# Value product in halves, causal mask of the probabilities on GpSimd, row maxima over two PSUM banks at once, exponentials from single banks

## The reference

```python
x = L0(x, c)   # quantised products and a gated scan, then an MLP
x = L1(x, c)   # attention, all keys;    then an MLP of width 512
x = L2(x, t)   # two small MLPs
x = L3(x, c)   # attention, causal mask; then an MLP of width 512

# attention in L1 and L3: 16 heads of 8 features
h = layernorm(x) * (1 + scale) + shift
q, k, v = split(h @ Wqkv)
s = q @ k.T / sqrt(8)
s = where(causal, s, -inf)          # L3 only
x = x + gate * (softmax(s) @ v) @ Wproj
```

## Time and profile before

| | us |
|---|---|
| median of 3 runs (495.15 to 497.51) | 497.06 |
| the profiled execution | 498.7 |
| its span | 496.6 |
| mean granted TensorE clock, share of full | 0.931 |
| loop of L1, first E to last copy of bank 6 | 198.1 to 301.5 |
| loop of L3, the same | 378.1 to 473.1 |

### The profile page before, as it was taken

How to read it: one execution, slowest core, us unless ns; L and a number is a source line. 1 busy time by engine, 2 the same in 40 slices (tenths; PEclk the granted TensorE clock), 3 DMA queues, 4 the chain that set the end, 5 groups by cost and what they waited for, 6 DMA issues and landing times.

```text
span 496.6 us, 6007 instructions
## 1 busy us (share of the span) xinstructions
PE 321.8 (65%) x2017; PEld 151.0 (30%) x2018; DVE 311.0 (63%) x787; ACT 242.7 (49%) x422; POOL 108.4 (22%) x160
## 2 busy tenths in 40 slices
PE   0025845621346463877777888867758999999886
PEld 0014523410115320121111224543412333334454
DVE  0778787859688568778888723335666555565230
ACT  3267556552564221466666685342422445555542
POOL 0112149632262510000000040173300000000410
PEclk9999999999999966599999999997965999999899
DMA  7940440000000332000000000000360000000001
GB/s 251 416 165 0 170 176 0 1 0 0 1 0 1 97 94 64 2 0 2 1 3 1 3 2 0 1 0 0 86 170 1 3 2 2 2 2 3 2 1 42
DMA packets 11650, 21.90 MB, mean 44 GB/s; under 512 B 2010, under 2 KB 10462, under 8 KB 10846
## 3 DMA queue, kind: packets, MB, share of 16 engines
q1 hardware_dynamic: 11620, 21.52, 12.6%
HBM read 14.57 MB, written 0.52 MB: 30 GB/s over the span
## 4 chain that ended last, share of the span: by engine, by line
PE 46%; DVE 26%; ACT 11%; issue 8%; POOL 6%; DMA 2%; SPq 0%; DVEq 0%; ACTq 0%; POOLq 0%
PE ps L1455 11%; PE ps L1437 7%; DVE nm L918 7%; PE pe L1477 4%; PE pe L1358 4%; PE ps L1510 4%; PE ps L1442 3%; POOL rstd L341 2%; PE pe L1480 2%; ACT scr L1130 2%; PE ps L1412 2%; DVE st L500 2%; ACT scr L1042 2%; PE ps L1229 1%; DMA big<-in_wa 1%
## 5 line engine op out<-in xcount | busy, mean ns | idle before, releaser
L918 DVE TENSOR_REDUCE nm<-ps 128x1 f32<-128x512 f32 (+2 forms) x224 | 135.0, 648 | 55.8 <-PE ps L1442 34.7
L1155 ACT ACTIVATE scr<-pe 128x1024 f32<-128x1024 f32 (+3 forms) x128 | 108.9, 866 | 102.5 <-PE pe L1480 59.2
L1437 PE MATMUL ps<-big 62*128 62x512 bf16 (+3 forms) x256 | 50.5, 386 | 36.3 <-DVE nm L918 32.6
L1455 PE MATMUL ps<-scr 128*32 128x512 f32 (+3 forms) x512 | 61.3, 552 | 6.2 <-ACT scr L1130 5.4
L341 POOL TENSOR_TENSOR rstd<-var,half 128x4 f32<-128x4 f32 x26 | 28.5, 1098 | 114.2 <-DVE var L505 88.2
L1477 PE MATMUL pe<-big 64*128 64x512 bf16 (+3 forms) x256 | 47.2, 367 | 1.1 <-ACT scr L1155 1.1
L425 POOL CAST nm<-nm 128x16 bf16<-128x16 f32 x16 | 3.2, 198 | 196.7 <-DVE nm L918 196.7
L1437 PEld LDWEIGHTS ps<-big 62*128 62x128 bf16 x256 | 14.5, 96 | 65.9 <-DVE nm L918 49.3
L1477 PEld LDWEIGHTS pe<-big 64*128 64x128 bf16 x256 | 12.5, 95 | 53.3 <-issue 24.9
L1358 PE MATMUL pe<-hT,w 128*128 128x512 f32 x48 | 24.6, 638 | 3.5 <-ACT hT L1109 3.5
L510 DVE TENSOR_SCALAR xn<-x_tok,mv,rstd 128x128 f32<-128x128 f32 x56 | 15.8, 344 | 13.6 <-POOL rstd L341 13.5
(11 more groups left out here) (221 smaller groups left out, 592.9 us busy)
## 6 DMA issues: line engine op xcount, KB each, us to landing
big<-tern SPq DMA_DIRECT2D x48, 128.0 KB, 2.4
big<-in_fill SPq DMA_DIRECT2D x1, 4096.0 KB, 13.6
big<-in_wa SPq DMA_DIRECT2D x1, 2304.0 KB, 12.5
w<-in_w SPq DMA_DIRECT2D x2, 1152.0 KB, 19.3
big<-in_wa SPq DMA_DIRECT2D x1, 1344.0 KB, 6.2
big<-in_w SPq DMA_DIRECT2D x1, 1024.0 KB, 14.3
w<-in_w SPq DMA_DIRECT2D x1, 896.0 KB, 20.0
rowg<-in_rowg SPq DMA_DIRECT2D x1, 832.0 KB, 18.3
```

What stands on the lines that cost most here:

```text
L918: v.tensor_reduce(dst, src[:, 0:w * len(pairs)].rearrange("p (h w) -> p h w", w=w), AX.X, ALU.max, negate=True).then_inc(sem(f"a{a}_max"), 1)
L1155: s_.activation(P[:, kt % 2, 2 * p:2 * p + 2, q0:S], E[(e - 1) % 2][:, :, q0:S], ACT.Exp, scale=SCALE).then_inc(sem(f"a{a}_p"), 1)
L1437: last = t_.matmul(dsts[par][:, k * wd:(k + 1) * wd], QZ[rows, b, 2 * g + i, qt * 128:(qt + 1) * 128], KZ[rows, b, 2 * g + i, 0:wd], start ...
L1455: last = t_.matmul(bank[6][32 * h:32 * h + 32, q0:S], V[b][:, kt, HG * g + h, :], P[:, kt % 2, h, q0:S], start=(kt == 0), stop=(kt == TB - 1),
```

## The change

**Rows maxima.** The banks become four pairs, and the ring two pairs, `RING = (0, 6)`: a round or any other item takes a pair. One reduction covers both banks of a round (128 x 2 x 512 to 128 x 2).

**Exponentials.** E writes single banks, `SINGLES = (2, 3, 4)` in turn, each product with its own wait and signal; ScalarE runs one exponential for each bank, 256 a layer where 128 were. `P` has four slots for key blocks (it had two) and lies where weights lay before.

**Values.** PV goes to bank 5, in two column halves, one in each step, three steps late in L1 and four in L3 (`LATE`); the first key block of a unit stays whole.

**Causal mask of the probabilities.** The product L1480 goes. GpSimd zeroes the part of the diagonal block above the diagonal in `P` with one `affine_select` (128 x 4 x 128) for each key block, 32 in all, and PV waits for it (`triangle`). GpSimd's queue is written out slot by slot of the schedule, the selections between the "parts".

**Around it.** `xn` of batch 0 is made by VectorE (four instructions), GpSimd's bias follows at slot 58, and "n_turn" moves from step 60 to 59.

```diff
+        TWO = [ctx.enter_context(nc.psum_tensor(f"pe{i}", [128, 2, 512], F32)) for i in range(4)]
+        E = TWO[1:3]
+        bank = [TWO[i // 2][:, i % 2, :] for i in range(8)]
...
-        P = scr[:, 0:2 * HG * S].rearrange("p (i h t) -> p i h t", i=2, h=HG)
+        P = wf32[:, NP * B * S:2 * NP * B * S].rearrange("p (i h t) -> p i h t", i=PRING, h=HG)
...
+        LATE = (3, 4)
+        EARLY = {52: "o_turn", 54: "proj", 59: "n_turn"}
+        COPIED, MODULATED, BIASED = 54, 61, 58
...
+        RING = (0, 6)
+        SINGLES, PV_BANK = (2, 3, 4), 5
...
+                    def lower_triangle(k):
+
+                        pool.wait_ge(sem(f"a{a}_p"), 4 * (k + 1))
+                        q0 = 128 * (k % TB)
+                        block_ = P[:, k % PRING, :, q0:q0 + 128]
+                        nc.gpsimd.affine_select(block_, block_, [[0, HG], [1, 128]], ALU.is_ge, zero, base=0,
+                                                channel_multiplier=-1).then_inc(sem("triangle"), 1)
+
+                    for k, slot in enumerate(schedule(n_max)):
+                        for item, u, *_ in slot:
+                            if item == "parts":
+                                maxima_parts(u)
+                            elif item == "proj" and u == 0:
+                                n_root(n + 1, 0)
+                        if causal and k >= 2 and k % 2 == 0:
+                            lower_triangle(k // 2 - 1)
+                        if k == BIASED:
                             add_bias(n + 1, 0)
...
-                            for par in range(2):
-                                src = bank[RING[ring % len(RING)]]
-                                ring += 1
-                                dve.wait_ge(sem(f"a{a}_ring"), ring)
-                                dst = nm[:, u % 2].rearrange("p (r i t) -> p r i t", r=2, t=TB)[:, par, pairs[0]:pairs[-1] + 1, qt]
-                                v.tensor_reduce(dst, src[:, 0:w * len(pairs)].rearrange("p (h w) -> p h w", w=w),
-                                                AX.X, ALU.max, negate=True).then_inc(sem(f"a{a}_max"), 1)
+                            src = TWO[RING[ring % len(RING)] // 2]
+                            ring += 1
+                            dve.wait_ge(sem(f"a{a}_ring"), ring)
+                            dst = nm[:, u % 2].rearrange("p (r i t) -> p r i t", r=2, t=TB)[:, :, pairs[0]:pairs[-1] + 1, qt]
+                            v.tensor_reduce(dst, src[:, :, 0:w * len(pairs)].rearrange("p r (h w) -> p r h w", w=w),
+                                            AX.X, ALU.max, negate=True).then_inc(sem(f"a{a}_max"), 1)
...
-                                act.wait_ge(sem(f"a{a}_sc"), e)
-                                if TB * u + kt >= 2:
-                                    act.wait_ge(sem(f"a{a}_pv"), TB * u + kt - 1)
-                                s_.activation(P[:, kt % 2, 2 * p:2 * p + 2, q0:S], E[(e - 1) % 2][:, :, q0:S], ACT.Exp,
-                                              scale=SCALE).then_inc(sem(f"a{a}_p"), 1)
+                                if TB * u + kt >= PRING:
+                                    act.wait_ge(sem(f"a{a}_pv"), 2 * (TB * u + kt - PRING + 1))
+                                for j in range(2):
+                                    i = 2 * (e - 1) + j
+                                    act.wait_ge(sem(f"a{a}_sc"), i + 1)
+                                    s_.activation(P[:, kt % PRING, 2 * p + j, q0:S], bank[SINGLES[i % 3]][:, q0:S], ACT.Exp,
+                                                  scale=SCALE).then_inc(sem(f"a{a}_p"), 1)
...
+                        mid = (q0 + S) // 2
+                        lo, hi = (q0, S if kt == 0 else mid) if part == 0 else (mid, S)
+                        if kt == 0 and part == 1:
+                            return
+                        if part == 0:
+                            if causal:
+                                pe.wait_ge(sem("triangle"), k + 1)
+                            else:
+                                pe.wait_ge(sem(f"a{a}_p"), 4 * (k + 1))
+                            if kt == 0 and u >= 1:
+                                pe.wait_ge(sem(f"a{a}_pvs"), u)
                         for h in range(HG):
-                            last = t_.matmul(bank[6][32 * h:32 * h + 32, q0:S], V[b][:, kt, HG * g + h, :],
-                                             P[:, kt % 2, h, q0:S], start=(kt == 0), stop=(kt == TB - 1),
+                            last = t_.matmul(bank[PV_BANK][32 * h:32 * h + 32, lo:hi], V[b][:, kt, HG * g + h, :],
+                                             P[:, k % PRING, h, lo:hi], start=(kt == 0), stop=(kt == TB - 1 and part == 1),
                                              tile_position=(0, 32 * h))
-                        last.then_inc(sem(f"a{a}_pv"), 1)
+                        last.then_inc(sem(f"a{a}_pv"), 2 if kt == 0 else 1)
...
-                        if s >= 2:
-                            pe.wait_ge(sem(f"a{a}_p"), s - 1)
                         for j in range(2):
+                            if 2 * s + j >= 3:
+                                pe.wait_ge(sem(f"a{a}_p"), 2 * s + j - 2)
                             rows = slice(HALF * j, HALF * j + HALF)
-                            last = t_.matmul(E[s % 2][:, j, q0:S], KZ[rows, b, 2 * g + p, kt * 128:(kt + 1) * 128],
-                                             QZ[rows, b, 2 * g + p, q0:S], start=True, stop=not causal)
-                        for j in range(2 * causal):
-                            last = t_.matmul(E[s % 2][:, j, q0:q0 + 128], cmask[:, 0], cmask[:, 2], start=False, stop=True)
-                        last.then_inc(sem(f"a{a}_sc"), 1)
+                            last = t_.matmul(bank[SINGLES[(2 * s + j) % 3]][:, q0:S], KZ[rows, b, 2 * g + p, kt * 128:(kt + 1) * 128],
+                                             QZ[rows, b, 2 * g + p, q0:S], start=True, stop=True)
+                            last.then_inc(sem(f"a{a}_sc"), 1)
                         for x in slots[s + 1]:
                             ring_item(*x)
-                        if p == 1 and s > 1:
-                            probs_out((s - 2) // 8, (s - 2) // 2 % 4)
-                    probs_out(7, TB - 1)
+                        if s >= LATE[causal]:
+                            probs_out((s - LATE[causal]) // 2, (s - LATE[causal]) % 2)
+                    for half_ in range(64 - LATE[causal], 64):
+                        probs_out(half_ // 2, half_ % 2)
```

More of the change, by code:

```diff
@@ L31 @@
 KROWS = 62
+PRING = 4
 WA_N = (D, 2 * ADA, ADC * D, OUT6, 6 * OUT6)
@@ L277, in ring_place @@
             before = ring_items[:ring_items.index(item)]
-            return len(before) + sum(x[0] == "max" for x in before)
+            return len(before)
         @block.sync
```

64 lines of the change are left out of this document (22 added, 42 removed).

## The result

The changed kernel takes **488.92 us** (median of four runs, 488.39 to 489.43), before 497.0 (495.15 to 497.51): a ratio of 0.985, 95% interval 0.982 to 0.987. The forecast was 470.0 with a range from 461 to 484. So the sign was right, and the size was not: 8 us came of the 27.

The account below looks back on a forecast made before the run. L1 was taken as bound by VectorE and the ring, L3 by TensorE. Terms of -3.5 - 9.3 + 0 - 3.0 - 1.5 - 9.3 - 0.5 = -27.1 us took 497.06 to 470.0 us, range 461 to 484.

Parts of the forecast that it names:

- L3, middle units: L3's five middle units: 9.95 us a unit in the place of 11.82, -9.3 us (-15 to -2).
- the masks: TensorE in L3: dropping the mask product saves 0.32 us a step, 8 x 0.32 = 2.56 us a unit.
- The halves: PV in L3: halves add three times the fixed price, and that of their rounding, 0.5 us a unit.
- The selections: GpSimd in L3: 1.27 us each, 6.0 us a unit, three steps of slack before PV; nothing in the middle.
- The stall of 1.2 us at the border: L3's unit border: ScalarE's copy waits for the last PV half, exponentials behind it; TensorE waits 1.2 us for E.
- Rival C: L3: TensorE loses its full clock, 6.1 us more a unit; six units at half clock give 507 us; chance 0.05.
- Rivals A and B: A: exponentials pace both loops, 482 us, chance 0.18. B: GpSimd's selections bound L3, middle 487 us, chance 0.07.
- L1, middle units: L1's five middle units: 10.85 us a unit in the place of 12.72, -9.3 us; bounds 10.0 and 12.0.
- the joint instruction: VectorE's reductions: one of 1024 columns adds 1.15 us in the place of 1.24 for two.
- L1, fill: L1's fill and first units: ten rounds by 0.3 us, -3.0, and PV halves -0.5; sum -3.5 us (0 to -5).
- L3's fill and first unit: L3's start: fill -3.0 us (0 to -4) as two pairs overlap; first unit -1.5 us (-3 to +1).
- The ends: Last steps of L1: 0 us (-2 to +2); last units of L3: -0.5 us (-2.5 to +6).

Follow-up runs that it names:

- e9: e6 with the two E products side by side first, then the two mask products: 482.66 us, ratio 0.973.
- e2: The changed kernel with PV three steps behind its exponentials in L3, not four (LATE = (3, 3)): 475.34 us, ratio 0.955.
- e4: The changed kernel plus useless products, overwritten at once, in TensorE's two border waits in L3, four in each: 481.97 us, ratio 0.970.
- e1: The changed kernel with L3's selections one step later in GpSimd's order, behind the casts of the maxima: 475.06 us, ratio 0.958.
- e3: The changed kernel with both edits, L3's PV three steps behind and selections one step later in GpSimd's order: 475.26 us, ratio 0.954.
- e7: e3 with `out` of the unit before moved in L3 from step 5 to step 7, which has no round: 470.42 us, ratio 0.948.
- e10: e3 with the halves undone in both loops, PV in one piece in every second step: 487.40 us, ratio 0.979.
- e12: e3 with PV four steps behind in L1, not three (LATE = (4, 3)): 480.87 us, ratio 0.968.
- e11: e3 with the joint reduction undone, two reductions of one bank each, pair given back after the second: 477.37 us, ratio 0.961.
- e6: e2 with the selections undone, the causal mask added by a second product in each E bank (product, mask, product, mask): 545.81 us, ratio 1.099.

## Why the prediction was wrong

**L3, middle units: the step that failed.** 9.95 us a unit were forecast and 13.2 came on average (66.02 / 5). The 3.25 us split in three. TensorE's work was 9.29 us, not 8.75: +0.54, because the masks had been priced at 2.56 us a unit, and e9 (11.39 busy) less e2 (9.46, above) is 1.93: the 0.32 us a step was read on a single step of 512 columns and taken for all eight. The halves cost about what was priced. Idle time was 2.56 us, not 1.2: +1.36. And the fall of the clock: the remaining 1.35, which e4 confirms as such.

Of the idle time, 0.95 us was forecast nowhere and goes back to one sentence. The selections were costed "at nothing in the middle", because "each selection has three steps before its PV asks for it". That is true of the one who waits for the selection, PV. It says nothing of what is queued behind it on GpSimd: the three casts, which `parts` waits for with all of TensorE behind it. GpSimd was busy for 3.10 us of 11.85, so its share showed nothing; the order did. The stall of 1.2 us at the border was right in kind and measured 0.89, but it holds the exponentials too, and through them the selection and so the casts. A further 0.72 us is no matter of GpSimd: the sum had no term in L3 for a ring of two pairs of which `out` takes one. It stays in e1; in e3 0.25 is left of it and in e7 nothing, though a wait of 0.48 for VectorE stands behind `parts` there. So 0.95 and 0.72 came on top, and 0.31 of the 1.2 did not come: +1.36. With the one order mended (e1) a unit takes 10.74 us at full clock, and the kernel 475 us, inside the range of 461 to 484. That the rest of the sum fits is in part luck: 5 us more than forecast came from the fill of L1, and about as much was lost at the two ends (below).

**Rival C was the right mechanism and had the wrong shape.** It was priced as a unit that runs at half clock as a whole, 6.1 us, and so got 0.05. In fact the clock falls for some 3 us at a border and comes back: 3.2 us in the first unit (15.04 against 11.85), nothing in the second, 0.9 to 1.4 in the next three, 1.35 on average. The row that spoke for it stood in the prediction: 0.92 of 2.00 us busy, and then 0.50. What spoke against it, L1's busy share of 75%, is a mean over a stretch without such a border: any two of its 2 us stretches side by side hold at least 2.5 us of 4, L3's borders 2.16. The rule of the Trainium skill that was cited there ("TensorE: Matmul & The Clock Gate", section "A second HAM failure mode: psum-queue depth-cycling") says that the clock swings in the gaps between groups when banks are cycled. The trace agrees in part, at four of L3's five borders, where the gaps are wide (1.11 and 1.05 us busy of 2.00 at one of them). In their middle units e3 and e7 cycle through the same banks in the same way and keep 1.00, so the cycling as such is not what does it here.

**Rivals A and B fell.** An exponential of 512 columns takes 0.60 us as forecast, and L1's steps are paced by reductions back to back (7.11 us for six), not by it. A selection takes 0.635 us, half of what was assumed, near the lower bound.

**L1, middle units: right.** 11.18 us, against 10.85 and bounds of 10.0 and 12.0; a reduction back to back costs 1.19 us and not 1.15, which over eight is 0.3 us, nearly all of the difference. E10 and e12 show its two reasons apart: the halves (1.25 us a unit) and a copy that does not hold E (0.34). The third reason, 0.09 us a round by the joint instruction, was over-sized three to six times (0.03 a round, 0.12 a unit; e11); what remains for the pairs is a ring of which one half is written while the other is read, which was not tried apart.

**L1, fill: the sign right, the size half.** -8.7 us against -3.5 with a bound of -5. The clock is the reason again, this time a gain. Before it is 0.50 until 213; after:

```profile
198.00:202.00 4.00, 3.80 (x20) 0.76 (x18) 3.05 (x4) 2.17 (x5) 0.61 (x3) 0.66 0.00 0
202.00:206.00 4.00, 3.46 (x38) 0.89 (x38) 3.63 (x5) 3.15 (x7) 0.00 (x0) 1.00 0.01 2
```

It reaches 1.00 some 12 us sooner. Up to the first E the span shortens by 3.4 us (198.11 to 194.75), near the 3.0 that were forecast for the rounds; from there to the first PV of unit 1 by another 5.4, where the forecast had 0.5 and kept all steps up to 213 at half clock. What brings the clock up sooner stays open, but it does so without two parts of the change: without the halves it is 0.96 from 202 to 206 (e10), and with two reductions a round 1.00 (e11). With PV four steps behind (e12) it rises at about 207. The stages before L1 ran at 1.00 in before's trace and mostly at 0.50 in this one; that plays no part, since e1's trace, at 1.00 there, has the copy of the PV bank at 209.52 and this one at 209.60.

**L3's fill and first unit: right** to 0.1 us (-2.9, -1.5). For the first unit this is in part luck: the half clock lasted 11.7 us from its first E on, before 9.0, and the rest of the unit made up for it.

**The ends: wrong by 1.6 us in L1 and 3.4 in L3.** In L3 the stretch over units 6 and 7 is longer than before's 17.54 (at 0.90) in every version of which the trace can tell. Its length goes with the clock: 18.38 in e3 and 18.42 in e9 at 1.00, 19.69 and 19.74 in e1 and e7 at 0.91, 20.49 in the changed kernel at 0.83, and 22.18 in e10 at 0.75. e3's:

```profile
426.34:444.72 18.38, 13.94 (x163) 6.48 (x161) 6.17 (x20) 11.02 (x31) 7.26 (x13) 1.00 0.01 1
```

So by e3 about 2 of the 3.4 us are again a fall of the clock, which the sum had left out. For the other 1.3, `proj`, the root and the turns now share two pairs, which is likely but was not tried apart; this stays open, as does L1's end.

## What to carry to other kernels

When work goes to an engine that is mostly idle, its busy share and the slack of its consumer are not enough. List what stands behind the new instruction in that engine's order, and who waits for that; here the order that made a wait of 0.95 us cost 14 us in all, since with it the clock fell at most borders too. A repeated border is priced in its own 2 us stretches, not by the mean of the loop. And two waits that share a cause do not add up: either edit alone brought 475 us, and both together no less.

## What was not expected of the hardware

- **The order of the same products decided the clock.** Product, mask, product, mask held TensorE at 0.50 for all of L3 with 48.00 of 48.00 us busy; the same products in pairs ran at 1.00 with 45.58 (e6, e9): 545.8 us against 482.7.
- **More work was faster.** Eight useless products a unit kept the clock and took 7 us off (e4).
- **The same border does not always cost the clock.** In the changed kernel 1.11 and then 1.05 of 2.00 us busy were followed by 0.50, but 1.20 and then 0.96, one border earlier and with the same waits, by 1.00. In e1 the clock stayed at 1.00 at four borders (1.11 and then 2.00 us busy at one of them), and fell at the fifth, with the same wait of 0.89 us.
- **Joining two reductions saves 0.03 us of 1.21** when they run back to back (e11).
- **A selection in place over 128x512 takes GpSimd 0.635 us**, half of its operation with two inputs of that size.
